# Gates of a mixture-of-experts layer: computed one step earlier and spread over partitions by DMAs through DRAM in place of TensorE matmuls

## What is computed

```python
n = layernorm(x)
agg = segment_sum(n[dst], src); count = edges per src   # mean over a node's edges
x = x + n @ W1.T + b1 + (agg / max(count, 1)) @ W2.T + b2

n = layernorm(x)
shared = mlp3(n)                                        # 256 -> 256 -> 128 -> 256, relu
all_out = 4 experts, each mlp3                          # 256 -> 128 -> 64 -> 256, relu
gates = softmax(n @ gW + gb)                            # 4 per node
topv, topi = top_k(gates, 2)
topw = softmax(topv)
x = x + shared + sum over the two of all_out[topi] * topw
```

## Time and profile before

| what | before |
|---|---|
| median of 3 runs | 3190.99 us (3190.84 to 3196.47) |
| the profiled execution | 3193.37 us |
| its span, first to last instruction | 3191.8 us |
| granted TensorE clock, mean over the span | 0.988 of full speed |
| busy: TensorE, VectorE, ScalarE, GpSimd | 97%, 84%, 61%, 58% |
| HBM traffic | 236.11 MB read, 161.00 MB written |

### The profile page before, as it was taken

The page is one execution under the profiler, slowest core; times in us unless marked ns, Lnnn a source line. Parts: engine busy times, 40 slices in busy tenths (PEclk is TensorE's granted clock), DMA queues, the critical chain, the costliest instruction groups (busy, mean ns, idle before and its releaser), DMA issues.

```text
span 3191.8 us, 61476 instructions
## 1 busy us (share of the span) xinstructions
PE 3083.1 (97%) x20817; PEld 2822.4 (88%) x20817; DVE 2671.9 (84%) x7211; ACT 1942.1 (61%) x3507; POOL 1842.0 (58%) x1554
## 2 busy tenths in 40 slices
PE   7999899999689999999999999999999999999998
PEld 7999899999678888889898989888888888888887
DVE  8988898885288888888888888888888888888886
ACT  5655565556455656565656566666666666666665
POOL 1788888888665555555555555555555555555540
PEclk9999999999899999999999999999999999999999
DMA  7777677777533333333333333333333333333320
GB/s 242 212 219 207 192 211 202 197 202 210 148 100 100 86 99 87 98 88 95 92 93 92 92 91 92 93 89 97 86 99 85 100 85 101 85 101 85 98 79 27
DMA packets 201824, 387.38 MB, mean 121 GB/s; under 512 B 106671, under 2 KB 109821, under 8 KB 201506
## 3 DMA queue, kind: packets, MB, share of 16 engines
q1 hardware_dynamic: 133906, 226.02, 26.0%
q10 hardware_dynamic: 30800, 102.42, 10.0%
q0 software_dynamic: 36800, 54.95, 7.4%
HBM read 236.11 MB, written 161.00 MB: 124 GB/s over the span
## 4 chain that ended last, share of the span: by engine, by line
PE 71%; POOL 1%; issue 0%; DVE 0%; ACT 0%; DMA 0%; POOLq 0%; DVEq 0%
PE acc L1127 25%; PE acc L1188 13%; PE acc L1097 13%; PE acc L1108 4%; PE acc L1110 4%; PE acc L1174 3%; PE acc L1151 3%; PE acc L1184 2%; PE acc L1143 1%; PE acc L1199 1%; PE acc L1137 1%; POOL rows L165 0%; DMA rows<-z_d,tab 0%; POOL e_oh L177 0%; ACT h2f L1232 0%
## 5 line engine op out<-in xcount | busy, mean ns | idle before, releaser
L165 POOL DMA_INDIRECT rows<-z_d,tab x500 | 580.2, 1160 | 612.7 <-DMA tab<-tab_d 478.7
L177 POOL TENSOR_SCALAR e_oh<-iota_sb,tab 128x250 fp32r<-128x250 f32 (+1 forms) x500 | 522.2, 1055 | 460.8 <-PE acc L1110 452.3
L1127 PE MATMUL acc<-x1T_hi,wl_hl 128*128 128x500 f32 x2400 | 665.4, 392 | 0.0
L386 POOL DMA_INDIRECT tab_d<-pair,idx x400 | 550.5, 1376 | 118.6 <-issue 112.0
L725 PE MATMUL acc<-w_hl,xT_hi 128*125 128x256 f32 x3200 | 575.1, 285 | 0.1
L1127 PEld LDWEIGHTS acc<-x1T_hi,wl_hl 128*128 128x128 f32 x2400 | 444.0, 188 | 84.0
L1188 PE MATMUL acc<-wl_hl,h_hi 128*125 128x256 f32 x2400 | 479.1, 282 | 0.0
L725 PEld LDWEIGHTS acc<-w_hl,xT_hi 128*125 128x125 f32 x3200 | 470.6, 190 | 0.0
L1389 DVE TENSOR_TENSOR h_lo<-h1f,h_hi 128x500 fp32r<-128x500 f32 x600 | 397.3, 676 | 48.9 <-ACT h_hi L1226 40.5
L1219 ACT ACTIVATE h1f<-acc,bl_sb 128x500 f32<-128x500 f32 x600 | 404.3, 674 | 14.4
L1188 PEld LDWEIGHTS acc<-wl_hl,h_hi 128*125 128x125 f32 x2400 | 391.8, 186 | 3.7
(11 more groups left out here) (144 smaller groups left out, 6384.5 us busy)
## 6 DMA issues: line engine op xcount, KB each, us to landing
xs<-in_x SPq DMA_DIRECT2D x100, 448.0 KB
z_d<-zs ACTq DMA_DIRECT2D x100, 448.0 KB
y_d<-ys ACTq DMA_DIRECT2D x100, 448.0 KB
y_sb<-y_d SPq DMA_DIRECT2D x100, 448.0 KB
x_sb<-in_x SPq DMA_DIRECT2D x100, 448.0 KB
out<-x_sb SPq DMA_DIRECT2D x100, 448.0 KB
codes_b<-code_d SPq DMA_DIRECT2D x25, 390.6 KB
rows<-z_d,tab POOLq DMA_INDIRECT x500
```

What stands on the lines that cost most here:

```text
L165: pool.indirect_dma_start(out=rows[g.h][:, q, :], out_offset=None, in_=z_d, in_offset=bass.IndirectOffsetOnAxis(ap=tab[g.h][:, q, 0:1], ax ...
L177: pool.tensor_scalar(e_oh[:, q, w], iota_sb[:, w], tab[g.h][:, q, 1:2].bitcast(F32), None, ALU.is_equal).then_inc(S["e_oh_ready"], 1)
L386: pool.indirect_dma_start(out=tab_d, out_offset=bass.IndirectOffsetOnAxis(ap=idx[:, n:n + 1], axis=0), in_=pair[:, 2 * n:2 * n + ROW], in_ ...
L1127: mm = pe.matmul(bank[L1_BANKS[t]][:, 0:GN], wl1_hl[:, w, f, t * P:(t + 1) * P], (x1T_hi, x1T_lo)[a][:, f, :], start=n == 0, stop=n == 5)
```

## The change

The gates of a group are computed one step earlier, and no longer pass through TensorE.

- TensorE: the four transposes of `wst` and the two selector matmuls are gone. The transposes of the logits (`logits_rows`) stand behind the first quarter of layer 3.
- VectorE: all gate functions run for group i+1 at the end of step i, behind the row blocks and between the statistics. The weights are kept as 16 columns ordered by expert and block; columns 16 to 31 are their high part and 32 to 47 their low part. `dve.transpose` turns `wst` (128 x 64) in blocks of 32 x 32 into `wst_T`. `gated` multiplies by `gbc`, which is in SBUF.
- ScalarE: the two exponentials stand at the step's end; the copy to `wT_r` is gone.
- SP: `spread_gates` stores `wst_T` in four pieces to `gate_d` in DRAM, waits for them, and loads from there each expert's 500 gates into 64 partitions of `gbc` (four loads) and the high and low rows into `wT_r` (two loads). It stands behind the y and x loads and ahead of the output store.
- In the first pass the constant `selg` is replaced by a two-column one (`low`), and a memset and a cast of `selg_r` are gone.

```diff
@@ -1074,3 +1075,8 @@
     gpair = sb("gpair", [SP_, NS, NX, NX], F32, c2)
-    wst = sb("wst", [SP_, NS, NB3], F32, c2)
+    wst = sb("wst", [P, 2 * 32], F32, c2)
+    wst_T = sb("wst_T", [P, 2 * 32], F32, c2)
+    gbc = [sb(f"gbc{t}", [P, GN], F32, c2) for t in range(2)]
+    w_own = wst[0:SP_, 0:16]
+    w_hi = wst[0:SP_, 16:32]
+    w_lo = wst[0:SP_, 32:48]
 
@@ -1102,2 +1108,11 @@
 
+        def logits_rows():
+            if front:
+                pe.wait_ge(S["x1_ready"], g.n(NS, 2))
+            pe.wait_ge(S["lgT_ready"], n1.n(1, 1))
+            for s in range(NS):
+                mm = pe.transpose(bank[5][0:SP_, s * P:(s + 1) * P],
+                                  lgT_sb[:, s * SP_:(s + 1) * SP_], ident_sb[:])
+            mm.then_inc(S["lgN_done"], 1)
+
         def sum_edges(k):
@@ -1132,14 +1147,3 @@
                 mm.then_inc(S["l1_done"], 1)
-            pe.wait_ge(S["gates_ready"], i.n(1, 1))
-            if i.c:
-                pe.wait_ge(S["out_ready"], i.n(2))
-            for s in range(NS):
-                mm = pe.transpose(bank[6][0:NB3, s * SP_:(s + 1) * SP_], wst[:, s, :],
-                                  ident_sb[0:SP_, 0:SP_])
-            mm.then_inc(S["wT_done"], 1)
             layer2(0)
-            pe.wait_ge(S["wT_ready"], i.n(1, 1))
-            for t in range(2):
-                pe.matmul(bank[6 + t][:, 0:GN], selg_r[:, t, :], wT_r[:],
-                          start=True, stop=True).then_inc(S["gate_bc_done"], 1)
             layer2(1)
@@ -1182,2 +1186,5 @@
                 if s == 0:
+                    pe.wait_ge(s_gw, i.n(32, 32))
+                    if i.c:
+                        pe.wait_ge(S["out_ready"], i.n(2))
                     pe.wait_ge(S["h2_lo_ready"], i.n(H2T, H2T))
@@ -1193,10 +1200,6 @@
                     mm.then_inc(S["l3_done"], 1)
-        if nxt:
-            if front:
-                pe.wait_ge(S["x1_ready"], g.n(NS, 2))
-            pe.wait_ge(S["lgT_ready"], n1.n(1, 1))
-            for s in range(NS):
-                mm = pe.transpose(bank[5][0:SP_, s * P:(s + 1) * P],
-                                  lgT_sb[:, s * SP_:(s + 1) * SP_], ident_sb[:])
-            mm.then_inc(S["lgN_done"], 1)
+                if s == 0 and nxt:
+                    logits_rows()
+        if nxt and not back:
+            logits_rows()
 
@@ -1244,13 +1247,4 @@
         if back:
-            act.wait_ge(S["gate_step"], i.n(4, 3))
-            act.activation(ga[:], z[:], ACT.Exp).then_inc(S["exp_ready"], 1)
-            h1_value(0)
-            h1_high(0)
-            act.wait_ge(S["gate_step"], i.n(4, 4))
-            act.activation(gy[:], gd[:], ACT.Exp).then_inc(S["exp_ready"], 1)
-            for t in range(1, H1T):
+            for t in range(H1T):
                 h1_value(t)
-                if t == H1T - 1:
-                    act.wait_ge(S["wT_done"], i.n(1, 1))
-                    act.copy(wT_r[0:NB3], bank[6][0:NB3, 0:GN]).then_inc(S["wT_ready"], 1)
                 h1_high(t)
@@ -1275,2 +1269,7 @@
             edges_high(act, i + 3)
+        if nxt:
+            act.wait_ge(S["gate_step"], n1.n(4, 3))
+            act.activation(ga[:], z[:], ACT.Exp).then_inc(S["exp_ready"], 1)
+            act.wait_ge(S["gate_step"], n1.n(4, 4))
+            act.activation(gy[:], gd[:], ACT.Exp).then_inc(S["exp_ready"], 1)
 
@@ -1320,9 +1319,11 @@
         if i.c:
-            dve.wait_ge(S["wT_done"], i.n(1))
-        gate_step(dve, i, 11, dve.tensor_tensor(gd[:], gd[:], r4, ALU.mult))
-        gate_step(dve, i, 12, dve.tensor_copy(wst[:, :, 0:NX].bitcast(F32R), gd[:]))
-        dve.tensor_copy(wst[:, :, 2 * NX:3 * NX].bitcast(F32R), gd[:])\
-           .then_inc(S["gates_own"], 1)
-        dve.tensor_tensor(wst[:, :, NX:2 * NX], gd[:], wst[:, :, 0:NX],
-                          ALU.subtract).then_inc(S["gates_ready"], 1)
+            dve.wait_ge(S["gates_turned"], i.n(1))
+        gate_step(dve, i, 11, dve.tensor_tensor(
+            w_own.rearrange("p (e s) -> p s e", s=NS), gd[:], r4, ALU.mult))
+        gate_step(dve, i, 12, dve.tensor_copy(w_hi.bitcast(F32R), w_own))
+        gate_step(dve, i, 13, dve.tensor_tensor(w_lo.bitcast(F32R), w_own, w_hi,
+                                                ALU.subtract))
+        if i.c:
+            dve.wait_ge(s_gst, i.n(64))
+        dve.transpose(wst_T[:], wst[:]).then_inc(S["gates_turned"], 1)
 
@@ -1367,4 +1368,5 @@
 
-    def graph_stats(dve, g):
-        for k, s in enumerate(S_ORDER):
+    def graph_stats(dve, g, part):
+        for k in part:
+            s = S_ORDER[k]
             wait_alone(dve, S["x1_ready"], g.n(NS, k + 1))
@@ -1372,2 +1374,4 @@
                .then_inc(S["l2_st_ready"], 1)
+
+    def graph_means(dve, g):
         for k, s in enumerate(S_ORDER):
@@ -1393,5 +1397,5 @@
         def gated(t):
-            dve.wait_ge(S["gate_bc_done"], i.n(2, t + 1))
+            dve.wait_ge(s_gbc, i.n(64, 64))
             dve.wait_ge(S["h2_relu_ready"], i.n(H2T, t + 1))
-            dve.tensor_tensor(h2f[t][:], h2f[t][:], bank[6 + t][:, 0:GN],
+            dve.tensor_tensor(h2f[t][:], h2f[t][:], gbc[t][:],
                               ALU.mult).then_inc(S["h2_gated"], 1)
@@ -1404,3 +1408,3 @@
         if back:
-            gates_logits(dve, i)
+            h1_low(0)
         if front:
@@ -1408,7 +1412,3 @@
         if back:
-            gates_softmax(dve, i)
-            h1_low(0)
-            gates_rank(dve, i)
             h1_low(1)
-            gates_weights(dve, i)
             h1_low(2)
@@ -1442,3 +1442,15 @@
             graph_vector(dve, g, more)
-            graph_stats(dve, g)
+        if nxt:
+            gates_logits(dve, n1)
+        if front:
+            graph_stats(dve, g, (0, 1))
+        if nxt:
+            gates_softmax(dve, n1)
+        if front:
+            graph_stats(dve, g, (2, 3))
+        if nxt:
+            gates_rank(dve, n1)
+            gates_weights(dve, n1)
+        if front:
+            graph_means(dve, g)
         if back:
@@ -1467,2 +1479,29 @@
 
+    def spread_gates(sp, i):
+        wait_alone(sp, S["gates_turned"], i.n(1, 1))
+        if i.c:
+            wait_alone(sp, s_gbc, i.n(64))
+            wait_alone(sp, s_gw, i.n(32))
+        else:
+            wait_alone(sp, S["cleared"], 6)
+        for b in range(4):
+            n = min(32, SP_ - 32 * b)
+            sp.dma_start(gate_d.rearrange("c r p -> r c p")[:, :, 32 * b:32 * b + n],
+                         wst_T[32 * b:32 * b + 32, :].rearrange("r (c p) -> r c p", c=2)
+                         [:, :, 0:n]).then_inc(s_gst, 16)
+        wait_alone(sp, s_gst, i.n(64, 64))
+        if i.c:
+            wait_alone(sp, S["h2_gated"], i.n(2))
+            wait_alone(sp, S["l3_done"], i.n(2))
+        for e in range(NX):
+            sp.dma_start(gbc[e // 2][e % 2 * 64:e % 2 * 64 + 64, :],
+                         gate_f[e * GN:(e + 1) * GN].partition_broadcast(64))\
+              .then_inc(s_gbc, 16)
+        sp.dma_start(wT_r[0:2 * NX].bitcast(F32),
+                     gate_f[NX * GN:3 * NX * GN].rearrange("(k n) -> k n", n=GN))\
+          .then_inc(s_gw, 16)
+        sp.dma_start(wT_r[2 * NX:3 * NX].bitcast(F32),
+                     gate_f[NX * GN:2 * NX * GN].rearrange("(k n) -> k n", n=GN))\
+          .then_inc(s_gw, 16)
+
     def step_sync(sp, i, more):
@@ -1472,2 +1511,4 @@
             load_y(sp, i + 4)
+        if (i + 1).exists():
+            spread_gates(sp, i + 1)
         if i.exists():
```

More of the change, by code:

```diff
@@ L63, in build @@
 def build(nc, x, src, dst, w1t, w2t, b12, wl1, bl1, wl2, bl2, wl3, b3, gw, gb,
-          ident, iota, codes, selg, tie, out, y_d, z_d, code_d, tab_d, tabx_d,
-          agg_x, cnt_x):
+          ident, iota, codes, low, tie, out, y_d, z_d, code_d, tab_d, tabx_d,
+          agg_x, cnt_x, gate_d):
     with ExitStack() as ctx:
@@ L114, in build @@
         s_store = [sem(f"out_stored{h}") for h in range(U)]
+        s_gst = sem("gates_stored")
+        s_gbc = sem("gates_spread")
+        s_gw = sem("gate_rows_loaded")
+        gate_f = gate_d.rearrange("c r p -> (c r p)")
         names = ("e_hi_ready e_lo_ready e_oh_ready agg_done cnt_ready deg_ready inv_ready "
@@ L117, in build @@
                  "x1n_ready x1T_done x1T_hi_ready x1T_lo_ready lgT_done lgT_ready lgN_done "
-                 "gate_step gates_own exp_ready gates_ready wT_done wT_ready l1_done "
-                 "h1_relu_ready h1_hi_ready h1_lo_ready gate_bc_done l2_done h2_relu_ready "
+                 "gate_step gates_own exp_ready gates_turned l1_done "
+                 "h1_relu_ready h1_hi_ready h1_lo_ready l2_done h2_relu_ready "
                  "h2_gated base_ready h2_hi_ready h2_lo_ready l3_done out_ready cleared").split()
@@ L203, in build @@
                 st_b3b = sb("st_b3b", [NB3, D], F32, c0)
-                st_sel = sb("st_sel", [NB3, 3, P], F32, c0)
+                st_low = sb("st_low", [NB3, 2], F32, c0)
                 st_b = sb("st_b", [1, 2, D], F32, c0)
@@ L346, in _ @@
```

(22 more changed lines are left out.)

9 lines of the change are left out of this document (3 added, 6 removed).

## The result

The change made the kernel slower by 0.3%: 3201.86 us in the median of 9 runs (3198.13 to 3209.99) against 3191.97 us in 9 runs of the kernel before on the same chip; the ratio is 1.0034 with a 95% interval of 1.0026 to 1.0043. Forecast were 3111 us and a faster kernel. The profiled execution took 3207.65 us, its span 3206.1 us.

A forecast was written before the change was run, and what follows sets the result against it. TensorE was taken to bound the second pass, before and after: 22.90 - 0.89 + 0.06 = 22.07 us per step, 81 us over about 98 steps, less 1.2 at the start, giving 3111 us; range 3099 to 3160.

The forecast's parts named there:

- The matmuls: TensorE, second pass: dropping four gate transposes (0.43 us) and two selector matmuls (0.46) saves 0.89 us per step.
- The transpose on VectorE: VectorE, end of step: the added 128x64 transpose of the gates takes 0.25 us, range 0.2 to 0.4.
- The round trip: Gates through DRAM on SP's queue: 8 issues of 0.40 plus 2 landings of 2.2, 7.6 us, fitting its room.
- The landings of 1.8 us more each: Gate DMAs under the Trainium skill's high-load HBM rule: 3358 us instead of 3111; on a rival way of chance 0.06.
- The 8.7 of room: Time from turned gates (23.9) to the next step's gating multiply (32.6): 8.7 us, 1.1 to spare.
- rival 2: Gate DMAs' trip ends between 8.7 and 9.5 us: step 22.1 to 22.9, 3125 to 3185 us; chance 0.06.
- the walk: VectorE's new order, each instruction at the later of its engine and operands, then DMAs and GpSimd's gathers and one-hots.
- All hidden: GpSimd's later gathers (12.3 to 19.3), one-hots (to 24.6) and reciprocal root (3.7 of next step) delay no engine.
- durations of before: VectorE's instructions in the new order keep their old times; gate arithmetic stays 3.7 us, slack under 1 us.
- rival 3: VectorE becomes the bound through a 0.4 us transpose and new waits: step 22.2 to 22.4, 3120 to 3145 us; chance 0.12.
- The touch of the logit transposes: TensorE's logit transposes, behind layer 3's first quarter, meet VectorE's second row block at 18.1: 0.06 us per step.
- the sum said 22.07: Forecast step time: 22.90 - 0.89 + 0.06 = 22.07 us, a gain of 0.83 per step.

The follow-up runs named there:

- the fastest version: Changed kernel plus table load ahead of the gate DMAs, one semaphore per half of the gate loads, logit transposes written over bank 4: 3124.0 us, ratio 0.9767.

## Why the prediction was wrong

**The matmuls:** right. 0.86 us per step were measured for 0.89.

**The transpose on VectorE:** right, 0.24 us for 0.25.

**The round trip:** right in its sum, in part by luck. The chain of waits has both landings (start, us), the SP queue's timeline the issues:

```profile
1959.39 1.51 DMA gate_d<-wst_T
1962.69 3.01 DMA gbc<-gate_d
```

```profile
2003.71 2.02 SPq L1489 DMA_DIRECT2D gate_d<-wst_T  x4
2006.82 2.37 SPq L1497 DMA_DIRECT2D gbc<-gate_d  x4
```

The chain counts a landing from the start of the last issue: 1.5 and 3.0 us. The prediction counted from its end, and so counted the timeline has 1.1 us from the stores (2005.73 to 2006.82) and at most 2.4 from the loads (2009.19 to 2011.57), for 2 x 2.2. An issue took 0.5 to 0.6 us for 0.40. The issues were put 1.2 us too low and the landings 0.9 too high, and so 7.9 us pass from the first store's issue to the multiply (2003.71 to 2011.57) where the sum had 7.6. The landings of 1.8 us more each, which the prediction weighed among its rivals, did not come. The 8.7 of room was right as well: in the fastest version 8.66 us lie between the transpose of the gates (2011.33) and the multiply (2019.99). But rival 2, a trip at the edge of its room, was real behind the first bound, through the shared semaphore that made the first multiply wait for the second half's loads. That cost 17 to 19 us.

**The step that failed** is the last of the walk: "the one-hots (5 x 1.06) to 24.6 ... All hidden". The one-hots were put at 19.3 to 24.6 of a step (they lie at 21.1 to 26.2), the gate instructions at 18.8 to 23.9. Both stood in the text, and the overlap came as written, only later (the one-hots by 1.8 us, the first gate instruction by 0.8). But I asked only who waits for the one-hots. I priced the gate instructions "with the durations of before", that is, of a place with no GpSimd beside them; in their new place they cost 1.57 us more. About 0.5 us of VectorE's idle time takes some of it (in the fastest version VectorE waits 0.41 before the last `h_lo` and 0.10 before the multiply), and the rest is the step's: by this estimate 22.07 + 1.57 - 0.5 = 23.1, and 22.93 were measured without the trip and 23.03 with it. So rival 3, VectorE as the bound, is what happened, but by a load that I had not put on it, and its price of 0.1 to 0.3 us per step was at most a third of the 0.96 by which the step missed 22.07.

**The touch of the logit transposes:** its place was right and its size was not. 0.06 was charged; the weight-load wait alone is 17.3 us in 94 steps, 0.18 per step, and taking the touch away gave 19 us by the ratios.

With these two taken away and the semaphore split, the step is 22.075 us where the sum said 22.07. That they agree so closely is partly chance: the matmuls gave 0.03 us less than the sum had, and the 0.06 charged for the touch is no longer in the step.

## What to carry to other kernels

A duration belongs to its place: before an instruction is priced at its old time, look at what the other engines do beside it in the old place and what they will do in the new one. When a step is put into a queue ahead of another, follow what that one feeds to the engine that runs it and to what runs beside it, not only to who waits for it. A bound that is removed may hide others of nearly the same length, so take them off one at a time, and where two consumers share a semaphore, ask which of them needs less than the whole count.
